# Value product of a gated cross-attention kernel, issued in two halves of 256 queries on either side of the last maximum matmuls of a key tile

## What is computed

```python
attn = jnp.einsum('bhqd,bhkd->bhqk', q, k) * scale
attn_w = jax.nn.softmax(attn, axis=-1)
out = jnp.einsum('bhqk,bhkd->bhqd', attn_w, v)
x = x + jnp.tanh(g_xattn[0]) * (out.transpose(0, 2, 1, 3).reshape(B, S, D) @ Wo.T + bo)
```

## Time and profile before

| | us |
|---|---|
| median of 3 runs (653.94 to 654.77) | 653.94 |
| the profiled execution's own time | 654.14 |
| its span in the trace | 652.0 |
| TensorE matmuls busy | 590.6 |
| TensorE weight loads busy | 279.8 |
| VectorE busy | 545.6 |
| ScalarE busy | 441.4 |
| GpSimd busy | 248.9 |

### The profile page before, as it was taken

How to read it: one execution, slowest core, us unless ns; L and a number is a source line. 1 busy time by engine, 2 the same in 40 slices (tenths; PEclk the granted TensorE clock), 3 DMA queues, 4 the chain that set the end, 5 groups by cost and what they waited for, 6 DMA issues and landing times. The chain is left out here.

```text
span 652.0 us, 19315 instructions
## 1 busy us (share of the span) xinstructions
PE 590.6 (91%) x6670; PEld 279.8 (43%) x6670; DVE 545.6 (84%) x952; ACT 441.4 (68%) x822; POOL 248.9 (38%) x375
## 2 busy tenths in 40 slices
PE   4998888799999999999999999999999994788485
PEld 2655554134334444444444444444444442333263
DVE  3788789899998999899899899899899636598887
ACT  2566666237777777677678767768777772688694
POOL 4978779600222541222213204204204210599400
PEclk9998999669999999999999999999999998799988
DMA  7777785532322232322223124124311000000024
GB/s 242 250 206 219 211 230 157 138 83 56 81 65 58 77 67 49 63 74 59 52 69 75 49 60 86 50 49 81 65 49 51 3 3 0 2 0 1 1 97 163
DMA packets 61255, 55.21 MB, mean 85 GB/s; under 512 B 11040, under 2 KB 58784, under 8 KB 61216
## 3 DMA queue, kind: packets, MB, share of 16 engines
q1 hardware_dynamic: 61216, 54.70, 32.1%
HBM read 37.62 MB, written 16.78 MB: 83 GB/s over the span
## 5 line engine op out<-in xcount | busy, mean ns | idle before, releaser
L834 ACT ACTIVATE prob<-st_ps 128x512 f32<-128x512 f32 x512 | 279.6, 599 | 109.9 <-PE st_ps L662 107.1
L885 DVE TENSOR_REDUCE negm<-mx_ps 128x1 f32<-128x512 f32 x512 | 321.7, 682 | 36.2 <-PE mx_ps L671 32.3
L671 PE MATMUL mx_ps<-k,q 96*32 96x512 bf16 x2048 | 211.4, 396 | 5.4 <-PEq L310 3.1
L662 PE MATMUL st_ps<-q,k 98*32 98x512 bf16 x2048 | 204.8, 383 | 0.1
L684 PE MATMUL pv_ps<-prob,v_u 128*32 128x512 f32 x1024 | 133.4, 592 | 0.3 <-ACT oT L847 0.2
L671 PEld LDWEIGHTS mx_ps<-k,q 96*32 96x32 bf16 x2048 | 57.7, 96 | 110.4 <-DVE negm L885 72.7
L1037 POOL TENSOR_TENSOR msplit<-negm,onesf 128x16 bf16<-128x16 f32 x32 | 7.1, 222 | 234.7 <-DVE negm L885 224.8
L662 PEld LDWEIGHTS st_ps<-q,k 98*32 98x32 bf16 x2048 | 59.2, 96 | 73.8 <-ACT prob L834 32.0
L297 POOL TENSOR_TENSOR parts<-work 128x512 bf16<-128x512 f32 x32 | 36.6, 1152 | 15.6 <-DVE work L285 14.1
L684 PEld LDWEIGHTS pv_ps<-prob,v_u 128*32 128x32 f32 x1024 | 32.8, 110 | 17.6 <-issue 0.8
L1290 ACT ACTIVATE wf<-banks,gscale 128x512 f32<-128x512 f32 x44 | 30.0, 695 | 10.3 <-PE banks L1251 4.4
(11 more groups left out here) (133 smaller groups left out, 748.9 us busy)
## 6 DMA issues: line engine op xcount, KB each, us to landing
qk_parts<-parts SPq DMA_DIRECT2D x96, 128.0 KB, 2.4
k<-qk_parts SPq DMA_DIRECT2D x192, 64.0 KB, 2.7
q<-qk_parts SPq DMA_DIRECT2D x192, 64.0 KB, 2.9
ctx<-in_ctxT SPq DMA_DIRECT2D x8, 512.0 KB, 5.0
X<-in_x SPq DMA_DIRECT2D x8, 512.0 KB, 6.2
out<-X SPq DMA_DIRECT2D x7, 512.0 KB, 2.9
q<-mrow SPq DMA_DIRECT2D x64, 4.0 KB, 2.5
wf<-in_w_down SPq DMA_DIRECT2D x1, 704.0 KB, 5.6
```

Source lines behind the costliest of these rows:

```text
L662: last = nc.tensor.matmul(st_ps[bank(i)][lo:lo + COLS, :], k6[g][:, h, kt * P + lo:kt * P + lo + COLS], q6[g][:, h, :], start=True, stop=True)
L671: last = nc.tensor.matmul(mx_ps[bank(i)][lo:lo + COLS, :], q6[g][0:ROWS, h, qt * P + lo:qt * P + lo + COLS], k6[g][0:ROWS, h, :], start=Tr ...
L834: nc.scalar.activation(prob[kt % 2][:, h, :], st_ps[bank(HPU * kt + h)][:], ACT.Exp, scale=SCALE).then_inc(exp_done, 1)
L885: nc.vector.tensor_reduce(negm[g % 2][:, h * TPB + qt:h * TPB + qt + 1], mx_ps[bank(TPB * h + qt)][:], op=ALU.max, axis=AX.X, negate=True) ...
```

## The change

The value product takes an argument `half` and multiplies 256 of the 512 queries in a call. The first half stands where the whole stood; the second is issued behind the last S and Q of the tile. The waits are in the first half, the increment of `pv_done` in the second. The flag that starts an accumulation is set in the first half of the first tile alone.

```diff
-                def weigh(b, g, kt):
+                def weigh(b, g, kt, half):
                     u = UPB * b + g
-                    pe.wait_ge(exp_done, 16 * u + HPU * (kt + 1))
-                    if kt == 0:
+                    cols = slice(half * S // 2, (half + 1) * S // 2)
+                    if half == 0:
+                        pe.wait_ge(exp_done, 16 * u + HPU * (kt + 1))
+                    if kt == 0 and half == 0:
                         pe.wait_ge(v_unit, u + 1)
                         if not (is_first(b) and g == 0):
                             pe.wait_ge(oT_ready, u)
                     for h in range(HPU):
-                        last = nc.tensor.matmul(pv_ps[32 * h:32 * h + 32, :], v_u[g % 2][:, kt, h, :], prob[kt % 2][:, h, :],
-                                                start=(kt == 0), stop=(kt == TPB - 1))
-                    last.then_inc(pv_done, 1)
+                        last = nc.tensor.matmul(pv_ps[32 * h:32 * h + 32, cols], v_u[g % 2][:, kt, h, :], prob[kt % 2][:, h, cols],
+                                                start=(kt == 0 and half == 0), stop=(kt == TPB - 1), skip_group_check=True)
+                    if half:
+                        last.then_inc(pv_done, 1)
...
+                            before = (b, g, kt - 1) if kt else (b, g - 1, 3) if g else (b - 1, 3, 3)
                             for h in range(HPU):
-                                if h == HPU - 1:
-                                    if kt:
-                                        weigh(b, g, kt - 1)
-                                    elif not (is_first(b) and g == 0):
-                                        weigh(*((b, g - 1) if g else (b - 1, 3)), 3)
+                                if h == HPU - 1 and (kt or not (is_first(b) and g == 0)):
+                                    weigh(*before, 0)
                                 scores(b, g, kt, h)
                                 if ahead:
                                     query_scores(mb, mg, kt, h)
+                            if kt or not (is_first(b) and g == 0):
+                                weigh(*before, 1)
...
-                weigh(B - 1, 3, 3)
+                for half in range(2):
+                    weigh(B - 1, 3, 3, half)
```

## The result

The change takes the median from 653.94 to 691.87 us (690.8 to 693.14, six runs): a ratio of 1.0571, with a 95% interval of 1.0547 to 1.0594. The direction was forecast, the size was not: +37.9 us against +5.95, and outside the range of 652.0 to 663.5.

The account below looks back on a forecast made before the run. It took TensorE as the bound, with VectorE nearly as full. Terms 0.6 + 3.5 + 0.35 + 0.2 + 1.3 - 0.7 + 0.7 = +5.95 us gave 659.9 us; own range 656.5 to 663.5, overall 652.0 to 663.5.

Parts of the forecast that it names:

- Instructions: Value product in every tile: four groups of half width take 0.865 against 0.860 us, +0.6 us in all, bounds 0 and 1.8.
- Rival C: Value product: the added weight loads are not hidden behind matmuls, 28 us by its count, total 688; chance 0.03.
- Q15 on its limit: Unit's last Q matmul group, units 2 and 3, batches 1 to 6: waits for VectorE's read two groups back; +0.29 each, +3.5 us.
- the list of signs: Closing list of what would show it right, including Q15 waiting about 0.4 and Q14 0.1 us in units 2 and 3.
- forecast 51.3: Sign for one batch in the middle of the kernel: it takes 51.3 us instead of 50.72.
- Unit 1: Unit 1 from batch 2, six units: VectorE's largest-value step delays Q15, and the half follows; +0.35 us in all.
- batch 0: First batch, VectorE-bound: the half behind Q15 makes units 1 to 3 each 0.43 us longer; +1.3 us.
- the last two units: End of kernel, without Q: the half follows the last S, which waits for ScalarE; +0.43 and 0.27, together +0.7 us.
- Rival B: Output transposes: they need no drain behind the half, total 652.1 us, chance 0.08; the reverse gives 668, chance 0.04.
- Rival A: Every tile: the earlier last Q uses VectorE's idle time, so Q15 and all other waits go; total 650.9 us, chance 0.10.

Follow-up runs that it names:

- run 3: Against the change: both halves of the value product put back where the whole one stood, in the loop, so only instructions are added; 682.04 us, ratio 1.0396.
- run 1: The change with TensorE's batch loop written out, eight bodies in a row and no branch back; 657.56 us, ratio 1.0042.
- run 2: The kernel before, value product whole, with TensorE's batch loop written out; 652.34 us, ratio 0.9965.
- run 8: The change with halves only in the first three key tiles of each unit, last tile whole in its old place, and TensorE's loop written out; 650.40 us, ratio 0.9948.
- run 9: The change with halves only in each unit's first key tile, plus batch 0's second tile, so the loop begins 64 records later than without that; 653.65 us.
- run 10: The kernel before with batch 0's first-key-tile value products as halves in their old place, 48 records more ahead of an untouched loop; 700.24 us, ratio 1.0691.

## Why the prediction was wrong

**The step that failed** is the first of the sum, *Instructions*: 0.6 us, with bounds of 0 and 1.8, and "The cover is the loading of weights beside matmuls". It asked what an added matmul costs to execute, and that answer holds: 0.01 to 0.02 a unit in run 3, or 0.3 to 0.6 us in 32 units. It never asked what it costs to have 16 more records in each tile of a loop. The bound was no bound, since the row that it rested on, the projection, runs inside a loop that stays loaded. The page of the kernel before showed 23 blocks fetched for the whole program; its trace shows none between 231 and 491 us, the five turns in which the loop was already there. Read as a resource, that line asks how far the loop is from not fitting. By the count above it was six records. What the added instructions cost was 33.0 us, at five branches back, and no rival had this mechanism. The rest, 5.2 us, is what the order costs (runs 1 and 2). So the forecast direction is borne out by those two runs and not by the result, most of which has a cause that the prediction did not name.

**Rival C** came near in us (688) by luck, with another mechanism. Loads are not in the open: a half takes 0.44 to the next S in the kernel after (281.55 to 281.99).

**What held**, read in run 1, where no branch disturbs it. The kernel of run 1, unit 3 and the start of unit 0:

```profile
288.63 0.39 PE L662 MATMUL st_ps<-q,k 98*32 98x512 bf16 x4
289.16 0.40 PE L671 MATMUL mx_ps<-k,q 96*32 96x512 bf16 x4
289.39 0.61 PE L686 MATMUL pv_ps<-prob,v_u 128*32 128x256 f32 x8
289.93 0.66 PE L735 MATMUL misc_ps<-ident,oT 128*128 128x128 f32 x4
...
301.30 0.66 PE L735 MATMUL misc_ps<-ident,oT 128*128 128x128 f32 x4
```

- Units 2 and 3 wait 0.31 at Q15 and 0.13 at Q14 (forecast: Q15 on its limit, which is 0.42 for both together by the sum; the list of signs gives 0.4 to Q15 alone, which is not what its own sum says). They take 13.47 us each, against 13.13 and 13.25 in run 2: 0.34 and 0.22, where the sum had 0.29 each, less 0.12 for one of them.
- A batch takes 11.37 + 12.95 + 13.47 + 13.47 = 51.26 us; forecast 51.3. (Unit 1 lost 0.06, forecast 0.05; six times that is 0.30, and the sum has 0.35.)
- In batch 0 the output transposes of units 1 and 2 start at 162.51 and 174.65, 12.14 apart; forecast 12.14 (11.71 + 0.43).
- In the last two units 0.41 and 0.27 are lost against run 2; forecast 0.43 and 0.27. Behind the last unit 0.18 comes back (2.47 instead of 2.65), which the forecast did not have.
- Ahead of a transpose a half leaves the gap that Q leaves: 0.32 from its second group (282.97 in the kernel after) to 283.29. Rival B, either way, is out.
- The sum of all this was +5.95; runs 1 and 2 differ by 5.2, and their attention by 5.1.

**Rival A**, the smoother order, was right about one place: in unit 1 the wait at Q15 falls if the product is split in the tile ahead of it (run 8). In the change itself this gain is lost again at the same Q15, since the second half stands behind it.

**How the 33 us divide** can be read for one branch but was not tried apart. At 297 us: 3.3 of waiting for the first block (3.50 from the last transpose to S, less the usual 0.21), 1.7 for 3.4 us at half clock, and a second short wait of 0.3 add up to 5.3, where the unit lost 5.1. The others lose more where the clock stays low longer: behind the branch at 469 us it is low for 10.2 us (471.49 to 481.73), the second wait splits a group by 1.21 us instead of 0.51, and the unit lost 8.4. Whether that part would vanish if TensorE had other work in the gap is open.

## What to carry to other kernels

Where an engine's loop is long, look at the instruction queue of the page and at the times of its fetches before pricing an edit: if fetching stops while the loop turns, the loop stays loaded, and any instruction added in the loop or anywhere ahead of it can end that, at 4.5 to 9.7 us a branch back here. Count the blocks that the loop touches, not its length. Moving its begin (run 9) and writing it out (run 1) both took the cost away here. Near the edge, compare other edits with the loop written out, since a shift of 48 records alone was worth 45 us (run 10). And a half placed behind a matmul that waits for a buffer two back waits with it: split work in front of the waits, not behind.

## What the runs showed of the hardware

Three things were not expected. A loop of 1588 records of TensorE turned with no fetch, and the same loop moved by 48 records (run 10) waited twice a turn, with 3.2 to 3.6 us from matmul to matmul each time. Straight on, 51 and 59 blocks were fetched (runs 2 and 1), with no more than 0.57 and 0.85 between the starts of matmuls from 165 to 537 us. And 3.5 us without matmuls were followed by a granted clock of 0.56 over the next 3.9 us, in a stretch where TensorE had been at full clock and was busy again at once.
